# Moving a slot's folds behind the next slot's first tile, with a third column-hat buffer, in a fused convolution kernel

## The reference

```python
x = x + winograd_conv3x3(gn(x))                   # F(4x4, 3x3), weights given in the transformed domain
x = x + deform_conv(gn(x), prelu(conv3x3(gn(x)))) # 9 taps, 8 groups, bilinear samples at learned offsets
x = x + binary_residual_block(gn(x))              # 4 sign-weight 3x3 convs, one int8 1x1, batch norms, rounding
x = x + edge_conv_attention(gn(x))                # 3x3 conv + |vertical difference| 1x1, squeeze-excite
```

## Time and profile before

| | |
|---|---|
| Time, median of 3 runs (lowest to highest) | 4684.99 us (4672.83 to 4689.32) |
| The profiled execution, its own time | 4687.73 us |
| Its span, first to last instruction | 4685.9 us |
| TensorE matmuls busy | 4264.4 us (91%) |
| VectorE busy | 2932.8 us (63%) |
| ScalarE busy | 1812.5 us (39%) |
| GpSimd busy | 3263.5 us (70%) |
| DMA | 1024 MB, 219 GB/s |
| TensorE's granted clock, mean | 0.973 |

### The profile page before, as it was taken

How to read it: one execution, slowest core, us unless ns; L and a number is a source line. 1 busy time by engine, 2 the same in 40 slices (tenths; PEclk the granted TensorE clock), 3 DMA queues, 4 the chain that set the end, 5 groups by cost and what they waited for, 6 DMA issues and landing times.

```text
span 4685.9 us, 74289 instructions
## 1 busy us (share of the span) xinstructions
PE 4264.4 (91%) x24997; PEld 2037.6 (43%) x24997; DVE 2932.8 (63%) x5482; ACT 1812.5 (39%) x1991; POOL 3263.5 (70%) x3094
## 2 busy tenths in 40 slices
PE   2799999999999999999999999999999999999992
PEld 2344444444444444444444444444444444444440
DVE  4556666666656766666666656665666666656552
ACT  1343434344434433434344334434434344334331
POOL 1777777777777767777676777767777676767740
PEclk8899999999999999999999999999999999999995
DMA  4577877877878686777768777686777868778752
GB/s 104 197 232 214 240 232 221 236 223 227 235 222 240 208 245 215 231 235 224 237 215 240 222 222 230 212 244 209 237 230 220 237 214 243 219 218 244 219 185 66
DMA packets 479569, 1024.32 MB, mean 219 GB/s; under 512 B 261924, under 2 KB 298116, under 8 KB 474628
## 3 DMA queue, kind: packets, MB, share of 16 engines
q1 hardware_dynamic: 325636, 516.15, 38.7%
q10 hardware_dynamic: 55296, 302.01, 18.6%
q0 software_dynamic: 98304, 201.52, 15.5%
HBM read 864.66 MB, written 73.99 MB: 200 GB/s over the span
## 4 chain that ended last, share of the span: by engine, by line
PE 57%; DVE 16%; DMA 11%; SPq 9%; issue 6%; ACT 1%; ACTq 0%; POOL 0%; DVEq 0%; POOLq 0%
PE ps_r L1445 40%; SPq L410 6%; DMA col_hat<-coord_table 5%; PE ps_c L1431 4%; DVE col_hat L1154 4%; PE ps_y L1457 4%; DMA wino<-xn_a 3%; PE ps_a L1384 2%; DVE ring L1165 2%; PE ps_a L1431 2%; DMA taps_c<-plane_act 2%; PE ps_t L1471 1%; DVE ring L1169 1%; DVE values L1175 1%; PE ps_y L1478 1%
## 5 line engine op out<-in xcount | busy, mean ns | idle before, releaser
L593 POOL DMA_INDIRECT ring<-patch_table,idx_part x3072 | 3254.9, 1060 | 1258.8 <-issue 1049.5
L1445 PE MATMUL ps_r<-select,image 128*128 128x512 f32 x6912 | 3166.2, 606 | 73.9 <-issue 47.7
L1445 PEld LDWEIGHTS ps_r<-select,image 128*128 128x128 f32 x6912 | 1273.7, 192 | 1526.1 <-issue 1490.2
L1154 DVE TENSOR_TENSOR col_hat<-ps_r,col_hat 128x512 f32<-128x512 f32 x1152 | 793.4, 689 | 1530.1 <-PE ps_r L1445 1201.1
L643 ACT ACTIVATE select<-row_in,minus_row 128x1536 f32<-128x1536 f32 x384 | 605.0, 1575 | 765.3 <-PE ps_r L1445 698.5
L645 ACT ACTIVATE select<-select,one_col 128x1536 f32<-128x1536 f32 x384 | 605.3, 1576 | 12.5
L1165 DVE TENSOR_TENSOR ring<-ring,w_cur 128x768 f32<-128x768 f32 x512 | 487.2, 952 | 15.2 <-DMA ring<-patch_table,idx_part 13.2
L662 ACT COPY samples<-ps_t 128x512 f32<-128x512 f32 x256 | 149.6, 585 | 886.7 <-PE ps_t L1471 886.7
L1457 PE MATMUL ps_y<-col_hat,w_dense 128*32 128x128 f32 x9216 | 379.4, 279 | 100.8 <-DVE col_hat L1154 94.9
L1457 PEld LDWEIGHTS ps_y<-col_hat,w_dense 128*32 128x32 f32 x9216 | 215.8, 109 | 307.5 <-DVE col_hat L1154 160.7
L1169 DVE TENSOR_TENSOR ring<-ring 128x384 f32<-128x384 f32 x512 | 283.2, 553 | 4.4
(11 more groups left out here) (231 smaller groups left out, 2362.5 us busy)
## 6 DMA issues: line engine op xcount, KB each, us to landing
row_in<-coord_table ACTq DMA_DIRECT2D x384, 768.0 KB
col_hat<-coord_table SPq DMA_DIRECT2D x384, 768.0 KB
ring<-patch_table,idx_part POOLq DMA_INDIRECT x3072
taps_c<-plane_act SPq DMA_DIRECT2D x144, 268.1 KB
taps_c<-xn_c SPq DMA_DIRECT2D x192, 130.0 KB
coord_table<-wino SPq DMA_DIRECT2D x64, 216.0 KB
wino<-xn_a SPq DMA_DIRECT2D x96, 130.0 KB
plane_act<-act_c SPq DMA_DIRECT2D x192, 65.0 KB
```

Source lines behind the costliest of these rows:

```text
L593: nc.gpsimd.indirect_dma_start(out=ring[j][:, h % 2, k, :], out_offset=None, in_=table, in_offset=bass.IndirectOffsetOnAxis(ap=idx_part[:, ...
L1154: v.tensor_tensor(hat_t, ps_r[:, (s + t) % 2], hat_t, ALU.mult).then_inc(tile_weighed, 1)
L1445: ins = mm(ps_r[:, (s + t) % 2], image[:, m, t], select[s % 2][:, m], start=(m == 0), stop=(m == PAIRS - 1))
```

## The change

Four parts:

1. On TensorE the folds of slot s - 1 (`fold_dense`, and the two `fold`s where e = 2) are issued inside slot s, behind its first row tile (`fold_before`). ScalarE's `save_conv` moves behind `make_select` and `place` in its slot, VectorE's `add_conv` from (0, 1) to (0, 2), and the first Winograd terms from (0, 2) to (0, 1).
2. `col_hat` has three buffers; in slot s SyncE asks for the columns of slot s + 2. The wait before it is still for the fold of slot s - 1. The columns of the next image's slot 0 are asked for in slot 22, behind the load of the image tiles.
3. The corner weights are written to `w_cur` directly at (22, 2); the copy in slot 23 goes, and `w_next` with it.
4. `values` holds the six gathered taps only; the second chunk is taps 2 to 5, with zero weights for 2 and 3.

```diff
+def chunk_start(k):
+    return min(4 * k, GTAPS - 4)
...
-        w_next = sb("w_next", [P, Q, GTAPS, CORNERS])
-        col_hat = [sb(f"col_hat{b}", [P, WT, HALF]) for b in range(2)]
+        col_hat = [sb(f"col_hat{b}", [P, WT, HALF]) for b in range(3)]
-        values = sb("values", [P, 2, JB, 4 * CHUNKS, C])
+        values = sb("values", [P, 2, JB, GTAPS, C])
...
 SyncE, load_cols
-                if not known_zero(n) or s >= 2:
-                    sp.wait_ge(dense_folded, (n * SLOTS + s - 1) * WT)
+                if not known_zero(n) or s >= 3:
+                    sp.wait_ge(dense_folded, (n * SLOTS + s - 2) * WT)
...
 SyncE, slot
-                if live(n + (s + 1) // SLOTS):
-                    load_cols(n + (s + 1) // SLOTS, (s + 1) % SLOTS)
+                ahead = s + 2
+                if live(n + ahead // SLOTS) and s != SLOTS - 2:
+                    load_cols(n + ahead // SLOTS, ahead % SLOTS)
...
                     a(n + 1, s)
+                    if s == SLOTS - 2:
+                        load_cols(n + 1, 0)
...
 ScalarE, slot
-                if e == 0 and live(before[0]):
-                    save_conv(*before)
                 if s != SLOTS - 2:
                     rows_ahead(n, s)
...
                     place(n, g + 2)
+                if e == 0 and live(before[0]):
+                    save_conv(*before)
...
 VectorE
-                if at == (0, 2):     # Winograd terms, first half
+                if at == (0, 1):
...
+                    if not known_zero(n):
+                        dve.wait_ge(weighted, n * Q + RING)
-                        ins = v.tensor_tensor(w_next[:, :, :, i], ...
+                        ins = v.tensor_tensor(w_cur[:, :, :, i], ...
...
-                            if live(n):
-                                dve.wait_ge(weighted, m * Q + RING)
-                            chain.step(v.tensor_copy(w_cur[:], w_next[:]))
...
-                if at == (0, 1):
+                if at == (0, 2):
                     add_conv(n)
...
 TensorE
                     if live(n):
                         row_tile(n, s, q)
+                    if q == 0:
+                        fold_before(n, s)
+                    if live(n):
                         if e == DT - 1 and q != 1:
                             turn(n, g, q // 2)
...
-                if live(n):
-                    fold_dense(n, s)
-                    if e == DT - 1:
-                        for k in range(CHUNKS):
-                            fold(n, g, k)
+            def fold_before(n, s):
+                n, s = (n, s - 1) if s > 0 else (n - 1, SLOTS - 1)
+                if not live(n):
+                    return
+                fold_dense(n, s)
+                g, e = divmod(s, DT)
+                if e == DT - 1:
+                    for k in range(CHUNKS):
+                        fold(n, g, k)
```

More of the change, by code:

```diff
@@ L303, in build @@
         row_in_in = [sem(f"row_in_in{b}") for b in range(2)]
-        col_hat_in = [sem(f"col_hat_in{b}") for b in range(2)]
+        col_hat_in = [sem(f"col_hat_in{b}") for b in range(3)]
         gathered = [sem(f"gathered{j}") for j in range(RING)]
@@ L455, in load_cols @@
                 part = coord_table[bass.ds((n % 2) * ITEMS + (dense_tap(e) * PARTS + g), 1), 2 * PAIRS * HALF:]
-                if not known_zero(n) or s >= 2:
-                    sp.wait_ge(dense_folded, (n * SLOTS + s - 1) * WT)
+                if not known_zero(n) or s >= 3:
+                    sp.wait_ge(dense_folded, (n * SLOTS + s - 2) * WT)
                 if s == 0:
                     sp.wait_ge(coords_out, n * COORDS_OUT + COORDS_OUT)
-                sp.dma_start(col_hat[s % 2][:].rearrange("p t x -> p (t x)"),
+                sp.dma_start(col_hat[s % 3][:].rearrange("p t x -> p (t x)"),
                              part.rearrange("o (w x) -> o w x", w=WQ).to_broadcast([C, WQ, WT * HALF])
-                             ).then_inc(col_hat_in[s % 2], 16)
+                             ).then_inc(col_hat_in[s % 3], 16)
             def load_image(n):
@@ L833, in prepare_rest @@
                 chain.step(v.memset(by_chunk, 0.0))
-                for t in range(4):
-                    ts = slice(t * C, (t + 1) * C)
-                    chain.add(v.tensor_copy(by_chunk[ts, 0:len(range(t, GTAPS, 4))], raw_d4[ts, t:GTAPS:4, :]))
+                for k in range(CHUNKS):
+                    for t in range(4):
+                        ts = slice(t * C, (t + 1) * C)
+                        if chunk_start(k) + t >= 4 * k:
+                            chain.add(v.tensor_copy(by_chunk[ts, k], raw_d4[ts, chunk_start(k) + t, :]))
                 chain.join()
@@ L1134, in a @@
                             chain.join()
-                        ins = v.tensor_tensor(w_next[:, :, :, i], hat[:, i // 2, 0, :, 0:GTAPS],
+                        ins = v.tensor_tensor(w_cur[:, :, :, i], hat[:, i // 2, 0, :, 0:GTAPS],
                                               hat[:, i % 2, 1, :, 0:GTAPS], ALU.mult)
@@ L1150, in weigh_tile @@
                 if t == 0:
-                    dve.wait_ge(col_hat_in[s % 2], (n * (SLOTS // 2) + s // 2 + 1) * 16)
+                    dve.wait_ge(col_hat_in[s % 3], (n * (SLOTS // 3) + s // 3 + 1) * 16)
                 dve.wait_ge(rows_made, tile + 1)
-                hat_t = col_hat[s % 2][:, t]
+                hat_t = col_hat[s % 3][:, t]
                 v.tensor_tensor(hat_t, ps_r[:, (s + t) % 2], hat_t, ALU.mult).then_inc(tile_weighed, 1)
@@ L1174, in add_columns @@
                     dve.wait_ge(turned, (part - 1) * CHUNKS)
-                v.tensor_tensor(values[:, g % 2, j, 0:GTAPS, :], tile[:, :, 0:C], tile[:, :, C:2 * C], ALU.add
+                v.tensor_tensor(values[:, g % 2, j], tile[:, :, 0:C], tile[:, :, C:2 * C], ALU.add
                                 ).then_inc(weighted, 1)
@@ L1458, in fold_dense @@
                                  w_dense[:, DT - 1 - e].rearrange("p g o -> p (g o)"),
-                                 col_hat[s % 2][:, t, j * P:(j + 1) * P], start=(e == 0 and t == 0), stop=False)
+                                 col_hat[s % 3][:, t, j * P:(j + 1) * P], start=(e == 0 and t == 0), stop=False)
                     ins.then_inc(dense_folded, 1)
@@ L1471, in turn @@
                     ins = nc.tensor.transpose(ps_t[:, j * P:(j + 1) * P],
-                                              values[:, g % 2, j, 4 * k:4 * k + 4].rearrange("p k c -> p (k c)"), ident[:])
+                                              values[:, g % 2, j, chunk_start(k):chunk_start(k) + 4].rearrange("p k c -> p (k c)"), ident[:])
                 ins.then_inc(turned, 1)
```

## The result

The changed kernel took 4533.44 us (median of 4 runs, 4529.11 to 4544.03) against 4682.93 us for the kernel before (median of 4, 4672.83 to 4689.32): ratio 0.9685, 95% interval 0.9665 to 0.9706. It is 150 us or 3.2% faster. The profiled execution took 4534.8 us with a span of 4533.0.

The account below looks back on a forecast made before the run. TensorE was taken to bound the kernel, busy 265 of 280 us a period. 128 - 26 - 21 + 18 - 22 - 24 - 13 + 15 = 55 us gave a forecast of 4630 us, range 4545 to 4685.

Parts of the forecast that it names:

- All is kept: Rival: VectorE has slack, relu and norm1 move up, convolution waits don't grow; 165 us gained, 4520 us, chance 0.18.
- fold waits: TensorE's waits for the weighed tile at fold_dense all go: +128 us, bounds 95 and 161.
- slot 9: Slot 9's removed fold wait returns as a longer wait for the taps in slot 11: -26 us, bounds 0 and -26.
- slot 12: Its fold wait lies inside the 19.8 us from norm1 to the offset convolution: -21 us, bounds -15 and -21.
- slot 11's folds: Folds formerly ahead of slot 12 move inside the norm1 stretch, where TensorE waits anyway: +18 us, bounds 0 and 18.
- third buffer: VectorE's column waits go, and with them TensorE's 15.2 us: +15 us, bounds 10 and 40; slot 21 taken as 0.
- in place: VectorE's slot 23 copy, 9.5 us in all, goes where nothing waits for it: 0, bounds 0 and 9.
- What bounds the kernel: TensorE sets the length, busy 265 us of a 280 us period and idle some 15.
- The queue behind the wait: In slot 12 load_cols asks 3.9 us later, just ahead of the copies, landing them 1.5 us later: -22 us.
- The clock: Longer waits lower the granted clock: -24 us at the offset convolution, -13 us at the taps' wait in slot 11.

Follow-up runs that it names:

- the second transfer: Changed kernel plus one more 768 KB transfer in slot 12 ahead of the copies, to a spare HBM area nothing reads; ratio 0.9721 to the kernel before.
- part 2 undone: Changed kernel with two column buffers asked for one slot ahead, folds still deferred; ratio 0.9965 to the kernel before.
- part 1 undone: Changed kernel with folds at their own slots' ends and save_conv, add_conv and Winograd terms at old places; ratio 0.9929 to the kernel before.
- three moves, two periods in the body: Changed kernel, columns behind copies, offset convolution at (14, 2), edge halves before their wait, two periods per loop body; ratio 0.9723 to the kernel before.

## Why the prediction was wrong

It forecast 55 us and got 150. The rival "All is kept" (165 us, 4520, chance 0.18) came nearest. Point by point, measured per period by the starts, times 15:

| step | predicted | measured |
|---|---|---|
| fold waits | +128 | +145 (whole run) |
| slot 9, then slots 10 and 11 | -26, clock -13 | -10 (0.46 + 0.21) |
| slot 12, slot 11's folds, the queue, slot 14's clock | -21 + 18 - 22 - 24 = -49 | -12 (0.77 + 0) |
| third buffer, slot 21 included | +15 | +17 (0.55 - 0.12 + 0.38 - 0.14 + 0.47) |
| in place | 0 | 0 |
| the loop's turn | not in the sum | +13 (0.57 + 0.29) |

**What bounds the kernel: right.** TensorE runs the same instructions and its idle time fell.

**Fold waits: right, a bit small.** The bounds were 95 and 161 and the starts give 144.6 us; the middle was a fair guess. No wait of the row tiles took their place.

**Slot 9: its reasons failed, and its size is open.** It read a fixed distance, relu to taps' convolution, off one period, and that was the one with the longest wait of the middle ones. TensorE's timeline of before, slot 11 in other periods:
```profile
1927.36 1.50 PE L1431 MATMUL ps_c<-taps_c,w_signs 96*32 96x512 bf16 x24
2484.06 1.50 PE L1431 MATMUL ps_c<-taps_c,w_signs 96*32 96x512 bf16 x24 [1.20 <-DMA taps_c<-plane_act]
2762.72 1.50 PE L1431 MATMUL ps_c<-taps_c,w_signs 96*32 96x512 bf16 x24 [0.73 <-DMA taps_c<-plane_act]
3887.11 1.50 PE L1431 MATMUL ps_c<-taps_c,w_signs 96*32 96x512 bf16 x24
```
In most there is no wait, so there was slack to use up. Nor is the distance fixed: it was 16.1 us on average (15.5 to 18.7) where the period read has 17.2, and 15.35 in the changed kernel. And the relu did move up, from 7.60 to 7.27 us behind the start of its slot's last row tile. Something is given back, as the step said: 10 us by the starts, 0.9 to 2.0 us a period (14 to 30 us) by the periods with the folds of slots 7 to 9 put back, and by the ratios of those runs nearly all. So the 26 us of wait are within what the runs allow. The 13 us of clock on top did not come: slot 11 lost nothing at the low clock.

**Slot 12: right.** With its folds and slot 13's put back the time is the same; nothing is kept there. The distance from norm1 is the same on average, 20.70 us before and 20.77 after, though not in single periods (19.25 to 22.40 before); the convolution waited at its end in 13 of 14 periods.

**The queue behind the wait: this is the step that failed.** The prediction let the copies land 1.5 us later (-22 us); they landed 0.1 us later, 20.7 us behind norm1 in place of 20.6. The ask moved by 4.0 us, as worked out (3.9), and a transfer ahead of the copies does cost them 3.9 us. The fault was to charge a price for the move: the copies of before landed as late already, with the transfer asked 4 us earlier. The stretches around slots 11 to 14 of the changed kernel, in the columns of the earlier trace rows:
```profile
2419.00:2423.00 4.00, 3.35 (x31) 1.48 (x30) 2.04 (x3) 2.88 (x5) 3.08 (x4) 1.00 1.00 375
2423.00:2427.00 4.00, 4.00 (x47) 2.09 (x46) 2.69 (x5) 2.82 (x4) 3.39 (x3) 1.00 0.51 170
2443.00:2447.00 4.00, 4.00 (x22) 1.69 (x25) 1.60 (x3) 0.59 (x1) 3.09 (x4) 1.00 1.04 348
```
The DMA's gap stands 4 us later than in the earlier trace rows (0.64 and then 0.97 there, 1.00 and then 0.51 here), and the end is as full (in this period the convolution did not wait). Why a later ask lands the copies no later was not taken further apart.

**The clock: failed as a consequence.** It priced waits of 3 and 2 us that did not come. Both of its levels in slot 14 were too high, 1.6 us a period now and 3.2 then: 0.6 us was lost before, and 2.2 with the wait at 3.19 us (the second transfer). The difference of 1.6 us, which alone is in the sum, would have been right had the wait come.

**Third buffer: the sum about right, 17 in place of 15, its parts not.** The row tiles of slots 4 and 5 gave 6 us and not 15, and slot 21, put at nothing, 11 (edge differences 0.38 less 0.14, low clock 0.47). And its role was missed: it was priced against the kernel before, while the deferral alone would have made the columns late (part 2 undone: 0.35% only).

**The turn was left out.** Its wait and low clock fell by 0.9 us a period. TensorE's waits there in the kernel before, and then its own branch instruction at the turn, before and after (ns, lowest/median/highest):
```profile
PE ps_r L1445 <- issue: 47.7, 11, 4.9
PE ps_r L1445 <- ACT image L654: 10.8, 4, 3.8
```
```profile
L171 PEldq COMPARE_BRANCH x14: 83/4472/5045, 674.1 to 4313.1; - x14
L176 PEldq COMPARE_BRANCH x14: 83/6374/6888, 660.9 to 4169.9; - x14
```
The view of waits names ScalarE's image copy in all the turns of the changed kernel, but the trace says otherwise. In all 13 turns before and in 11 of 13 after, the first row tile starts 0.35 to 0.42 us behind the end of this branch, when ScalarE's first image copy has been done for 2.4 to 3.5 us (before) or 0.5 to 1.3 us (after). What changed is where the branch begins: on average 4.8 us ahead of that row tile before, as the last folds of the period were issued, and 6.8 us ahead after, while TensorE still worked through the last row tile and transposes. More of it is covered, though it lasts longer. The folds of slot 23, which now stand behind the turn, are the only thing on TensorE that moved there, and with the folds back at their slots' ends (part 1 undone) the turns wait 4.4 to 6.7 us. `save_conv` is not the reason: the image copies stand ahead of it in both kernels.

The measured terms add up to 153 us, which is what the two profiled executions differ by; the medians differ by 150. Of the 98 that the sum of the prediction lacks against them, slot 14 with the queue and its clock are 37, slot 9 and its clock 29 (by the starts), the fold waits 17, the turn 13 and the buffer 2.

## What to carry to other kernels

A distance between two events can be charged as a limit where the later engine waits at its end in nearly every period (13 of 14 at the offset convolution, 6 of 14 in slot 11): read it over all periods, and never from the one picked because it shows a wait. Before a moved transfer is charged with delaying another, ask whether it already does so where it stands now. And price a buffer together with the reordering that it comes with: here each alone brought under 1%, both 3.2%.

## What the runs showed of the hardware

The turn of the loop is dear. The first row tile behind it stands 3.8 to 4.9 us in the kernel before and 2.9 to 4.1 us in the changed one. TensorE's own taken branch lasts 4.0 to 5.0 us before and 5.2 to 6.9 us after; the last one, which leaves the loop, 0.08 us. The same holds with two image copies moved ahead of the turn: in all 13 turns the row tile starts 0.35 to 0.41 us behind the branch's end. The view names a wait for the last semaphore event ahead of it, which the branch's end is not, and so names ScalarE.

ScalarE loads its activation table anew at the top of the body (1.28 us). With one period in the body it does so 0.02 us after its last copy; with two (three moves, two periods in the body) it first stands 3.0 to 4.5 us without any instruction, and then the row tile follows its first image copy by 0.13 us: a turn costs 5.9 to 7.4 us in place of 3.5. So halving the number of turns won 12 us, within the noise, and 43 us once the copies were moved out of the turn's shadow. The Trainium skill (Runtime: NRT & Kernel Launch, section "Instruction fetch mechanics") says that a taken branch whose target is outside the window of fetched instructions forces a fetch by DMA before the engine goes on. The traces agree: TensorE, with some 3400 instructions in a period, stands at its branch for 4 to 7 us in every version looked at, and ScalarE, with some 350, only when the body is two periods long.

The clock's price grows faster than the wait. Over the same slot 14, a mean wait of the offset convolution of 0 us lost 0 us at the low clock, 1.75 us lost 0.6, 3.19 us lost 2.2. The first is the kernel with the columns behind the copies, the others the changed kernel and the one with the second transfer. In single periods the wait alone does not tell: in the changed kernel waits of 2.5 and 3.5 us were followed by a loss of 1.7 us each and one of 2.9 us by 3.0, but one of 2.8 us by none.
